# A chunked scan of 128 image rows: one product for each group of decay sums, another order of products, y normalised on ScalarE

## What is computed

```python
xBC = silu(conv3x3(xBC) + conv_b);  dt = softplus(dt + dt_bias)
dA_cs = cumsum(dt * A, axis=2)                       # within a chunk
Lmat = exp(dA_cs[:, :, :, None, :] - dA_cs[:, :, None, :, :])
att = where(causal, einsum('bcihn,bcjhn->bcijh', Ch, Bh) * Lmat * dt, 0)
y_intra = einsum('bcijh,bcjhp->bcihp', att, x)
new = carry * exp(dA_cs[-1]) + states                # over the chunks
y_inter = einsum('bcihn,bcih,bchpn->bcihp', Ch, exp(dA_cs), prev_states)
y = y_intra + y_inter + D * x
y = (y - mean(y)) / sqrt(var(y) + 1e-5) * norm_w + norm_b
out = (y * z) @ out_proj_w.T                         # z: the gate
```

## Time and profile before

| | |
|---|---|
| median of three runs | 2463.56 us (2460.02 to 2467.26) |
| the profiled execution | 2459.31 us |
| its span | 2457.5 us |
| mean granted clock of TensorE | 0.966 |
| busy over the span: TensorE, VectorE, ScalarE, GpSimd | 88%, 68%, 53%, 45% |
| `scan_rows` within it | about 852 to 1836 us |

### The profile page before, as it was taken

One profiled execution on the slowest core, in us unless ns is written; L12 is line 12 of the kernel. 1 busy time (PEld: TensorE's weight loads), 2 busy tenths in 40 slices (PEclk: granted clock), 3 DMA queues, 4 the chain that ended last, 5 costly groups with the idle time before them and its releaser, 6 DMA issues. The chain is left out here.

```text
span 2457.5 us, 64304 instructions
## 1 busy us (share of the span) xinstructions
PE 2165.3 (88%) x22969; PEld 1624.6 (66%) x23096; DVE 1662.4 (68%) x3164; ACT 1311.9 (53%) x2727; POOL 1109.5 (45%) x1392
## 2 busy tenths in 40 slices
PE   0699997998899399999999999999987999879998
PEld 0475645887788267777777777777766656356563
DVE  5355585665565578888888888888873555735557
ACT  0255540085047577777777777777743555334543
POOL 0333250000000168888778877878853322432325
PEclk9999997999999699999999999999998999989999
DMA  9624495415623422222222222222226045961459
GB/s 215 182 81 79 100 329 160 122 29 179 204 54 125 137 51 60 60 58 58 58 61 59 61 58 58 58 59 60 59 60 180 25 88 139 311 184 35 91 132 316
DMA packets 305629, 272.25 MB, mean 111 GB/s; under 512 B 175966, under 2 KB 238846, under 8 KB 299210
## 3 DMA queue, kind: packets, MB, share of 16 engines
q1 hardware_dynamic: 294698, 256.00, 37.5%
q0 software_dynamic: 9280, 6.44, 2.1%
q10 hardware_dynamic: 1496, 7.63, 1.0%
HBM read 165.29 MB, written 81.46 MB: 100 GB/s over the span
## 5 line engine op out<-in xcount | busy, mean ns | idle before, releaser
L1692 DVE TENSOR_TENSOR l_scan_att<-l_scan_decay,l_scan_causal_scores 128x512 f32<-128x512 f32 x384 | 330.2, 860 | 63.3 <-ACT l_scan_decay L1661 63.1
L715 ACT COPY l_arena<-l_body_bank 128x384 f32<-128x384 f32 x192 | 142.0, 901 | 262.3 <-PE l_body_bank L587 262.3
L1655 ACT ACTIVATE l_scan_decay<-l_scan_cum 128x512 f32<-128x512 f32 x384 | 216.3, 597 | 33.0 <-PE l_scan_cum L1547 32.9
L1661 ACT ACTIVATE l_scan_decay<-l_scan_decay 128x512 f32<-128x512 f32 x384 | 227.8, 630 | 4.1
L1672 ACT ACTIVATE l_scan_yw<-l_scan_y_by_channel,l_scan_norm_b,l_scan_norm_w 128x128 f32<-128x128 f32 x384 | 148.1, 456 | 125.5 <-PE l_scan_y_by_channel L1609 124.5
L1594 PE MATMUL l_scan_gate_projected<-l_scan_xr,l_wf 97*128 97x128 f32 (+1 forms) x1536 | 205.3, 283 | 1.4 <-DVE l_scan_xo L1747 1.2
L1625 PE MATMUL l_scan_gate_projected<-l_scan_yz,l_scan_wo 128*96 128x128 f32 x1536 | 198.5, 279 | 1.1 <-DVE l_scan_yz L1724 1.1
L567 POOL TENSOR_TENSOR l_arena<-l_arena 96x512 f32<-96x512 f32 x96 | 122.6, 1277 | 168.8 <-ACT l_arena L780 161.6
L1625 PEld LDWEIGHTS l_scan_gate_projected<-l_scan_yz,l_scan_wo 128*96 128x96 f32 x1536 | 170.9, 163 | 40.0 <-issue 29.6
L1512 POOL TENSOR_TENSOR l_scan_inter<-l_scan_inter,l_scan_xd 128x384 f32<-128x384 f32 x128 | 128.0, 1000 | 151.4 <-DVE l_scan_inter L1707 151.4
L1594 PEld LDWEIGHTS l_scan_gate_projected<-l_scan_xr,l_wf 97*128 97x128 f32 (+1 forms) x1536 | 181.0, 190 | 17.2 <-issue 2.2
(11 more groups left out here) (191 smaller groups left out, 4896.2 us busy)
## 6 DMA issues: line engine op xcount, KB each, us to landing
l_scan_xc<-convolved_rows SPq DMA_DIRECT2D x128, 224.0 KB, 2.8
x_after<-l_arena SPq DMA_DIRECT2D x64, 384.0 KB, 4.8
l_arena<-x_after SPq DMA_DIRECT2D x64, 384.0 KB, 5.6
convolved_rows<-l_slots SPq DMA_DIRECT2D x48, 441.0 KB
l_conv_x_main<-x_after SPq DMA_DIRECT2D x64, 256.0 KB, 2.8
l_arena<-x_after SPq DMA_DIRECT2D x16, 1024.0 KB, 8.7
prepare_xt<-x SPq DMA_DIRECT2D x8, 1536.0 KB, 9.3
l_arena<-x SPq DMA_DIRECT2D x32, 384.0 KB, 5.5
```

Source lines behind the costliest of these rows:

```text
L715: nc.scalar.copy(tA[:, b, :, j:j + 2].rearrange("p c q -> p q c"), bank[n % 4][:, 0:2 * C].rearrange("p (q c) -> p q c", q=2)).then_inc(t_ ...
L1655: nc.scalar.activation(decay[:, b % 2, 4 * g:4 * g + 4, :], cum[(b + g) % 2][:], ACT.Relu, scale=-1.0)\
L1661: nc.scalar.activation(group, group, ACT.Exp, scale=-1.0).then_inc(exp_done, 1)
L1692: nc.vector.tensor_tensor(att[:, b, 4 * g:4 * g + 4, :], decay[:, b % 2, 4 * g:4 * g + 4, :], causal[:, b % 2:b % 2 + 1, :].broadcast_to([ ...
```

## The change

In `scan_rows` the weights `pick` and `unpick` give way to `lift`, one copy of the spreading weights for each of the four buffers. Three small DMAs a turn write the row's own sums (three bf16 parts of 12 heads x 128) into three partitions of `lift` where `cum_t` is padded; the padding becomes -1, so that four products of 128 columns give `cum[i] - cum[j]` at once. TensorE waits for these DMAs ahead of a turn's group 0.

TensorE's list is reordered: group 0 and the transposition of B and C come first, the state product moves up behind `yi` (into other columns of its PSUM tile), inter and the scores follow, and group 1 stands behind the scores. ScalarE takes over yn, as an Identity with scale and bias behind its first exponential; VectorE makes the bias, minus mean times reciprocal deviation, a 128x1 product. VectorE's state and xo move up, each ahead of a product with the scores, and the output statistics are taken once in four rows, over 512 pixels. SyncE waits for the constants before its first load. The next layer reads a quarter of the statistics.

```diff
-                nc.gpsimd.memset(parts[:], 0.0).then_inc(padded, 1)
+                nc.gpsimd.memset(parts[:], -1.0).then_inc(padded, 1)
...
+                sp.wait_ge(ready, CONST)
...
+                        if not (isinstance(r, int) and r < U):
+                            hold(sp, cum_done, 3 * (r - 3), passed)
+                        for part in range(3):
+                            own = 64 * (b % 2) + 3 * N_HEADS + part
+                            first = 64 * (b % 2) + part * N_HEADS
+                            sp.dma_start(lift[own:own + 1, b], cum_t[first:first + N_HEADS, bass.ds(n * 2 + b // 2, 1), :])                                .then_inc(lift_landed[b], 16)
...
-                    heads = slice((b % 2) * N_HEADS + 4 * g, (b % 2) * N_HEADS + 4 * g + 4)
-                    nc.tensor.matmul(bank[:].rearrange("p h w -> p (h w)"), pair, unpick[:, heads, :].rearrange("p h w -> p (h w)"),
-                                     start=True, stop=False)
+                    if g == 0:
+                        pe.wait_ge(lift_landed[b], n * 48 + 48)
                     for h in range(4):
-                        last = nc.tensor.matmul(bank[:, h, :], pick[:, (b % 2) * N_HEADS + 4 * g + h, :], pair,
-                                                start=False, stop=(h == 3))
+                        last = nc.tensor.matmul(bank[:, h, :], lift[:, b, 4 * g + h, :], pair, start=(h == 0), stop=(h == 3))
...
                         pe.wait_ge(state_ready, r + 1)
+                        for g in range(2):
+                            last = nc.tensor.matmul(p_i[g * N_STATE:(g + 1) * N_STATE, 0, half_s], xc[:, b, D_INNER:D_INNER + N_STATE],
+                                                    xw[:, b % 2, g * D_INNER // 2:(g + 1) * D_INNER // 2], start=True, stop=True)
+                        last.then_inc(st_done, 1)
...
+                    if row0:
+                        decays(0)
+                    if row3:
+                        r, b, n = row3
+                        act.wait_ge(turned, r)
+                        act.wait_ge(shift_done, r + 1)
+                        nc.scalar.activation(yn[:, b % 2], y[:, b % 2], ACT.Identity, bias=shift[:, b], scale=rstd[:, b]).then_inc(yn_done, 1)
...
-                        nc.vector.tensor_scalar(yn[:, b % 2], y[:, b % 2], mv[:, b, 0:1], rstd[:, b], ALU.subtract, ALU.mult)\
-                            .then_inc(yn_done, 1)
+                        nc.vector.scalar_tensor_tensor(out=shift[:, b], in0=mv[:, b, 0:1], scalar=-1.0, in1=rstd[:, b], op0=ALU.mult, op1=ALU.mult)\
+                            .then_inc(shift_done, 1)
...
+                        if b == U - 1:
+                            for kk in range(2):
+                                nc.vector.bn_stats(stats[:, kk, bass.ds(n, 1), :], xo[:, kk].rearrange("p u w -> p (u w)")).then_inc(stats_done, 1)
```

More of the change, by code:

```diff
@@ L1585, in turn @@
                             .then_inc(scores, 1)
+                        cumulative(row0, 1)
                     if row4:
@@ L1637, in turn, with gaps, decays @@
                     row0, row2, row3 = (at(lag) for lag in (0, 2, 3))
+                    def gaps(g):
+                        r, b, n = row0
+                        act.wait_ge(cum_done, 3 * r + g + 1)
+                        nc.scalar.activation(decay[:, b % 2, 4 * g:4 * g + 4, :], cum[(b + g) % 2][:], ACT.Relu, scale=-1.0)\
+                            .then_inc(gap_done, 1)
+                    def decays(g):
+                        r, b, n = row0
+                        act.wait_ge(gap_done, 2 + 3 * r + g + 1)
+                        group = decay[:, b % 2, 4 * g:4 * g + 4, :]
+                        nc.scalar.activation(group, group, ACT.Exp, scale=-1.0).then_inc(exp_done, 1)
+                    if row0:
+                        r, b, n = row0
+                        act.wait_ge(att_done, 3 * r)
+                        gaps(0)
+                        act.wait_ge(bc_turned, r + 1)
+                        if not (isinstance(r, int) and r < U):
+                            act.wait_ge(inter_done, r - 2)
+                        nc.scalar.copy(bct[0:N_STATE, b, 0, :], p_bcg[N_STATE:2 * N_STATE, 0, :])
+                        nc.scalar.copy(bct[:, b, 1, :], p_bcg[2 * N_STATE:4 * N_STATE, 0, :]).then_inc(bc_copied, 1)
                     if row2:
@@ L1685, in _ @@
                     .then_inc(ready, 1)
-                nc.vector.tensor_copy(pick[:], spread(spreads[:], 128)).then_inc(ready, 1)
-                nc.vector.tensor_scalar(unpick[:], spread(spreads[:], 128), -1.0, None, ALU.mult).then_inc(ready, 1)
+                for b in range(U):
+                    heads = slice((b % 2) * N_HEADS, (b % 2 + 1) * N_HEADS)
+                    nc.vector.tensor_copy(lift[:, b], spread(spreads[:, heads], 128)).then_inc(ready, 1)
                 dve.wait_ge(ready, CONST)
@@ L1726, in turn @@
                         r, b, n = row2
+                        if not (isinstance(r, int) and r < 2):
+                            dve.wait_ge(yn_done, r - 1)
                         dve.wait_ge(y_back, r + 1)
```

75 lines of the change are left out of this document (23 added, 52 removed).

## The result

The changed kernel takes **2439.29 us**, the median of 15 runs (2435.08 to 2444.82), against 2456.25 (2443.23 to 2467.26) for the kernel before in as many: a ratio of 0.9945 (0.993 to 0.996). It is faster by 0.55% (0.4 to 0.7%), a small gain. The prediction said 2376 and 2341 to 2428: the sign is right, the size is not. The profiled execution took 2443.12 us, with a span of 2441.1.

The account below looks back on a forecast made before the run. TensorE bounds the kernel at 7.53 us a turn; SyncE's chain of 6.65 plus 0.2 for statistics makes 6.8. Over 125 turns 91 less, 4 more at the start: 2376 us, range 2341 to 2428.

Parts of the forecast that it names:

- the paragraph on SyncE: SyncE's queue: third new copy issued 4.1 us after xo starts, landing 1.8 later, so TensorE goes on after 5.9.
- the chain: From turn start over xo, SyncE's loads and copies to the turn after next: 13.3 us for two turns, 6.65 each.
- the new DMAs are dearer: Rival on SyncE's copies: landing in 3.0 or 0.7 per issue, 7.1 to 7.4 a turn, 2414 to 2451 us; 12%.
- new rows that land after 2.5 us: Sign that the forecast is wrong: the DMAs of the new rows of weights land after 2.5 us.
- once in four behind the large statistics: Expected sign: `yi` 6.8 us apart on average, unevenly, the long turn once in four behind VectorE's 512-element statistics.
- The burst of statistics: VectorE's two 512-element statistics in the fourth turn delay the next `yi`: +0.8 us in four turns, 0.2 a turn.
- Four microseconds: Outside the turns: SyncE's wait for all constants before the first load adds 4 us at the start.
- Both parts of the argument: TensorE: removing products (-0.63 us a turn, +0.1 for a group's end) gives 7.0; fewer changes of form give 6.52.
- the layout of 6.52: TensorE's steps of one turn in the new order, laid out by the profile rows: 6.52 us.
- 6.3 said: Loop from one `yi` to the next through inter, VectorE's scaling and GpSimd's products: 6.3 us, TensorE following 0.05 after GpSimd.
- ScalarE's part: ScalarE with yn added: 5.4 us becomes 5.9 a turn of 6.8, priced at nothing.
- The fold of the next layer: Outside the turns: the next layer reads a quarter of the statistics, worth 0, at most -3 us.

Follow-up runs that it names:

- e2: Changed kernel with one DMA of 36 pieces into three partitions instead of three DMAs of 12 pieces: 2362.61 us, ratio 0.9634.
- e9: Changed kernel with each of the three copies at 16 pieces of 256 B instead of 12: 2394.16 us, ratio 0.9755.
- e6: e5 with the output statistics taken every row again (128 pixels, twice) instead of once in four rows: 2344.56 us, ratio 0.9561.
- e11: e6 with y by channel waiting only for GpSimd's first product and the state product for the second: 2315.07 us, ratio 0.9447.
- e12: e11 with `pick` and `unpick` kept and no copies, SyncE's store of xo placed as in the changed kernel: 2363.08 us, ratio 0.9649.
- e1: Changed kernel with SyncE's load of xr and store of xo one turn later in its list: 2364.73 us, ratio 0.9637.
- e3: Changed kernel with own sums copied for the first four rows only, later rows reusing them: 2362.36 us, ratio 0.964.
- e4: Changed kernel with `pick` and `unpick` products as before and no copies, new order kept: 2374.0 us, ratio 0.9672.
- e7: e4 with the transposition of B and C moved back behind y by channel: 2399.52 us, ratio 0.9775.
- e5: e1 with VectorE's 128x1 product moved behind the scaling of inter: 2362.14 us, ratio 0.9628.
- e13: e11 with yn back on VectorE, behind the scaling of inter: 2327.76 us, ratio 0.9505.
- e14: Kernel before with only the new order of the lists (products, statistics as before; no copies; yn on VectorE ahead of the scaling): 2411.84 us, ratio 0.9858.

## Why the prediction was wrong, point by point

**The failed step is the issue price of the copies in the paragraph on SyncE.** The prediction named the chain, its members and its start rightly: xo 7.4 after the turn's start (measured 7.21, 7.31 and 7.49), the landing 1.8 (measured 2.0). What it took from other DMAs is the issue: 0.6 for the first copy and 0.5 for each of the next two. Measured are 0.64, 0.96 and 0.89. The rest of the queue was a little dearer too: from xo to the second load of xc 2.60 where 2.5 was said, and 2.94 once in four turns, where SyncE's loop begins again. So from xo at 1411.39 the third copy is issued after 5.43, not 4.1, and TensorE goes on after 7.43, not 5.9. That two-turn chain is 14.64 instead of 13.3; over the pattern of four the turn is 7.33 instead of 6.65. Of the 0.68 between them the two steps from copy to copy are 0.43, the loads of xc and the landing 0.13 and 0.12. e2 and e9 bear this out: two issues less, or three shorter ones, and the time comes back. The rows gave prices for loads from memory and stores; for a copy inside SBUF with 12 pieces there was none, and the same duration was used with a tight interval round it. The rival "the new DMAs are dearer" had this as its condition (0.7 an issue and more, 7.1 to 7.4 a turn, 2414 to 2451) and 12%. It came true, and only its near part was in the range.

The sign given for it, new rows that land after 2.5 us, would not have caught it: they land in 2.0, and it is their issue that is late. The long turns are not once in four behind the large statistics, but every second one, behind the DMA. The Trainium skill, page "DMA: Bandwidth & Descriptors", section "Anatomy of one DMA", from which the prediction has a fixed 2.0 us, describes DMAs that GpSimd issues; that copies from SyncE's queue take 2.0 us too is what this trace shows.

**What that does to the sum.** 7.337 against 6.8 is 0.54 a turn, 67 us in 125 turns; the profiled execution is 71 above the 2372 said for it. The burst of statistics was counted on top of the chain (+0.2), but in the changed kernel it lies beside the wait: VectorE takes it from 1418.89 to 1420.16 and then still stands idle for 1.07 us ahead of the scaling at 1421.29. With the wait gone it costs 0.15 a turn (e6), near the 0.2 said. So the chain's own error of 0.68 came out smaller in the sum by what the burst doesn't add, and that is luck.

**The start.** Four microseconds were said; TensorE's first group of sums starts after an idle of 23.18 us where it was 19.95, and the first `yi` is 3.3 later. Not foreseen: the turns behind it are slow. The first seven take 59.0 us, 7.6 more than seven of the mean length; the third alone takes 10.72. The granted clock is lower there, 0.64 between 880 and 900 where the kernel before had 1.00; the row of before, then that of after:

```profile
880.00:900.00 20.00, 19.52 (x217) 15.61 (x213) 16.41 (x36) 14.51 (x32) 16.25 (x23) 1.00 0.26 58
```

```profile
880.00:900.00 20.00, 18.07 (x157) 16.03 (x156) 14.09 (x27) 13.70 (x29) 14.99 (x18) 0.64 0.16 36
```

Of the two levels, 1.2 and 2.4 GHz, this stretch of after is mostly at the lower; ahead of it stood the longer idle and turns with less work (12.6 of 20 us busy from 860 to 880, before 16.3). e11 shows the same (third turn 11.44), and so does e12 at full clock (11.83), so the clock isn't all of it. In the profiles of e1, e3 and e4 the third turn is 7.76, 7.75 and 6.77. What makes it long stays open.

**TensorE: right in kind, too small.** The order is worth 0.76 rather than 0.47 a turn (e4), a change of form 0.14 (e7; 0.1 to 0.15 said), and the products 0.63 of TensorE's time by the rows (e12 against e11 gives 0.38, with GpSimd as the limit). Both parts of the argument held; the layout of 6.52 was too cautious by 0.3 to 0.4. In e11 a group of sums takes 0.22 to 0.23 where 0.32 was laid out, three times a turn, the scores 0.31 for 0.41, inter 0.43 for 0.52, and all of TensorE's steps there add up to 6.18. These had been kept at the price they have between other forms. That the turns without a wait last 6.53 and 6.62 looks like the 6.52, but isn't: by e5 they are GpSimd's loop.

**GpSimd: named, 0.3 too short.** 6.3 said, 6.62 measured in e5. The largest part of it is the step from GpSimd's last product to TensorE, 0.30 instead of 0.05. No row shows the 0.05: in the kernel before `yi` starts 0.68 after GpSimd is through (1406.56 to 1407.24), so TensorE came late there and the step couldn't be read.

**ScalarE and VectorE.** yn takes 0.70 us on ScalarE, not 0.5, and releases nobody late. The move is worth 13 us (e13), and much more than that if it keeps yn from standing ahead of the scaling (e14). That the 13 us come from VectorE's shorter list is likely but wasn't shown. In the sum ScalarE's part stood at nothing, and what the move saves on VectorE was counted only as room. VectorE's 128x1 product is 0.15 (0.1 to 0.2 said).

**Outside.** The fold of the next layer gave 1.3 us at most, where 0 to 3 were said: between the first and last `yi` the changed kernel is 18.4 us shorter, at the start 3.3 longer, and the span 16.4 shorter, so 1.3 are left for everything else.

**The chances.** Half of the weight lay on one sum of three terms that each stood within 0.3 us of the next, with one of them resting on a price of a kind of DMA that no row showed. The prediction said itself that the chain sets the turn at 6.65 and put its upper end at 7.25; a range that reached to that end would have been 2341 to 2433, and with the rival's 7.4, 2451.

## What to carry to other kernels

A queue that issues DMAs is an engine with an order of its own: before adding a transfer whose consumer stands at the head of a turn, look at which wait stands ahead of it in the issuing queue, and put it ahead of those waits or put them a turn later. Here two numbers in SyncE's list were worth 75 us, over four times what the whole change brought. When an engine that was full is relieved, list the loops that close behind it and let each consumer wait only for what it reads: one such wait cost nothing while TensorE was full (e4 and e12 differ in it, and both have turns of 6.77) and was worth 28 us afterwards (e11).

## What the runs showed that I had not expected

- The issue of a copy inside SBUF: records of 0.74 to 0.82 us for 12 pieces, 0.81 for 36 pieces, 0.53 for 16 pieces, against 0.35 to 0.41 for loads and stores with memory in the same queue. A third more bytes were cheaper to issue.
- A change of the array's form costs 0.14 us in an fp32 stretch, and one instruction in the wrong place pays it twice (e7: 25 us in the whole kernel).
- From GpSimd's last product to the TensorE instruction that waits for it 0.30 us (e5). In the kernel before this step can't be read, since TensorE came 0.68 later and never waited.
- Statistics of 512 elements every fourth turn use less of VectorE and, once SyncE's wait is gone, cost 18 us more than 128 elements each turn (e6).
- SyncE's queue takes 0.34 us more where its loop begins again, once in four turns (0.43 in the kernel before), and in the changed kernel this lies on the chain.
